# Long attention steps taken head by head, and value products of one step at a time in two column quarters

## The reference, cut to what matters

```python
# x: (4, 512, 512); a cross attention over 64 context rows comes first, then this layer,
# then a second cross attention and a second mixture of 32 experts
def attention(x, kv_d_w, q_d_w, k_u_w, v_u_w, q_u_w, rope_k_w, rope_q_w, o_w):
    # q, k, v: 16 heads of 32, half of each rotary
    ...
    scores = jnp.einsum('bqhd,bkhd->bhqk', q, k) * scale
    scores = jnp.where(causal[None, None], scores, jnp.finfo(scores.dtype).min)
    probs = jax.nn.softmax(scores, axis=-1)
    out = jnp.einsum('bhqk,bkhd->bqhd', probs, v).reshape(b, s, H)
    return out @ o_w

h = x + attention(rmsnorm(x, ln1_w), ...)
out = h + moe(rmsnorm(h, ln2_w), ...)     # one shared and 7 routed experts, top 2
```

## Time and profile before

| | |
|---|---|
| median of the three runs | 2032.91 us (2032.46 to 2034.27) |
| the profiled execution | 2038.68 us, its span 2036.5 us |
| busy over the span | PE 1606.6 us, DVE 1354.6, ACT 1017.8, POOL 884.9 |
| mean granted clock of PE | 0.869 of 2.4 GHz |
| attention of `front`, first scores to last products | some 142 to 655 us of the span |
| one value-product record (L1047) | 273 ns, median of 1280 |

### The profile page before, as it was taken

The page is one execution under the profiler, slowest core; times in us unless marked ns, Lnnn a source line. Parts: engine busy times, 40 slices in busy tenths (PEclk is TensorE's granted clock), DMA queues, the critical chain, the costliest instruction groups (busy, mean ns, idle before and its releaser), DMA issues. The chain is left out here.

```text
span 2036.5 us, 33507 instructions
## 1 busy us (share of the span) xinstructions
PE 1606.6 (79%) x8846; PEld 1224.0 (60%) x8847; DVE 1354.6 (67%) x2659; ACT 1017.8 (50%) x1941; POOL 884.9 (43%) x654
## 2 busy tenths in 40 slices
PE   4568697797776669999947652199999999999991
PEld 3445565565455447777726441188888888878881
DVE  7645665565564456667656432189999999999992
ACT  1124534434343046666511100178888888888880
POOL 4100010110201222444413556557887888788881
PEclk8589998898888779999965555599999999999996
DMA  9144234242240253675562113268888888898778
GB/s 324 39 103 105 65 107 99 63 134 53 63 125 1 92 154 101 159 164 102 83 200 76 42 35 94 59 145 178 177 194 183 180 174 201 192 225 202 127 125 278
DMA packets 170842, 266.19 MB, mean 131 GB/s; under 512 B 21856, under 2 KB 97504, under 8 KB 169024
## 3 DMA queue, kind: packets, MB, share of 16 engines
q0 software_dynamic: 52624, 113.84, 28.8%
q1 hardware_dynamic: 118128, 151.24, 25.0%
HBM read 150.55 MB, written 87.33 MB: 117 GB/s over the span
## 5 line engine op out<-in xcount | busy, mean ns | idle before, releaser
L1544 DVE TENSOR_TENSOR moe_w_lo<-moe_w_up,moe_w_hi 128x1536 fp32r<-128x1536 f32 (+1 forms) x216 | 408.3, 1890 | 31.7 <-ACT moe_w_hi L1430 22.1
L1430 ACT ACTIVATE moe_w_hi<-moe_w_up 128x1536 fp32r (+3 forms) x216 | 343.1, 1589 | 20.5 <-SPq L1332 20.5
L1371 POOL DMA_INDIRECT moe_rows<-moe_rows,moe_ids x200 | 317.4, 1587 | 68.2 <-issue 56.4
L1639 PE MATMUL psum<-moe_w_hi,moe_rows_hi 128*128 128x384 f32 (+1 forms) x864 | 323.1, 374 | 18.4 <-DVE moe_rows_lo L1538 18.3
L1640 PE MATMUL psum<-moe_w_lo,moe_rows_hi 128*128 128x384 f32 (+1 forms) x864 | 304.1, 352 | 0.0
L1641 PE MATMUL psum<-moe_w_hi,moe_rows_lo 128*128 128x384 f32 (+1 forms) x864 | 303.7, 352 | 0.0
L1665 PE MATMUL psum<-moe_w_down,moe_hid_t 128*128 (+1 forms) x544 | 268.6, 592 | 1.8 <-DVE moe_tail_t L1532 1.2
L1387 POOL DMA_INDIRECT moe_sum<-moe_res,moe_ids x100 | 163.8, 1638 | 104.8 <-ACT moe_res L1467 54.6
L816 DVE TENSOR_REDUCE neg_top<-psum 128x1 f32<-128x128 f32 (+3 forms) x256 | 118.2, 484 | 126.1 <-PE psum L1028 125.9
L1387 POOL DMA_INDIRECT moe_other<-moe_res,moe_ids x100 | 162.6, 1626 | 88.2 <-ACT moe_res L1467 35.0
L1538 DVE TENSOR_TENSOR moe_rows_lo<-psum,moe_rows_hi 128x512 fp32r<-128x512 f32 x216 | 148.7, 689 | 54.8 <-issue 42.9
(11 more groups left out here) (270 smaller groups left out, 2925.1 us busy)
## 6 DMA issues: line engine op xcount, KB each, us to landing
moe_w_up<-in_L_ffn_w_gate SPq DMA_DIRECT2D x32, 384.0 KB
moe_w_up<-in_L_ffn_w_up SPq DMA_DIRECT2D x32, 384.0 KB
q_st<-q_hi SPq DMA_DIRECT2D x64, 128.0 KB, 2.6
k_st<-k_hi SPq DMA_DIRECT2D x64, 128.0 KB, 2.7
k_st<-k_lo SPq DMA_DIRECT2D x64, 128.0 KB, 2.7
q_st<-q_lo SPq DMA_DIRECT2D x64, 128.0 KB, 2.7
moe_w_down<-in_L_ffn_w_down SPq DMA_DIRECT2D x32, 256.0 KB
moe_w_down<-in_L_ffn_w_down SPq DMA_DIRECT2D x64, 128.0 KB
```

The lines of the kernel that those rows point to most:

```text
L1371: pool.indirect_dma_start(rows[u][:, :], None, d["rows"], bass.IndirectOffsetOnAxis(ids[:, t:t + 1], 0)).then_inc(gathered[u], 16)
L1430: sc.activation(w_hi[u % SPLITS][:, :], w_up[:, bass.ds(at * DC, DC), :].rearrange("p a n -> p (a n)"), ACT.Copy).then_inc(T["wh"], 1)
L1544: v.tensor_tensor(w_lo[u % SPLITS][:, :], w_up[:, bass.ds(at * DC, DC), :].rearrange("p a n -> p (a n)"), w_hi[u % SPLITS][:, :].bitcast(F ...
L1639: mm(ps[:, 2 + i, 0:2 * I], hi, w_h, start=(k == 0), stop=False)
```

## The change

A long step becomes two units, `(n, 0)` and `(n, 1)`, one a head; a short step stays one unit `(n, None)`. All three engines' lists now run over `UNITS`. The transposes of head 0 go to bank 4, which DVE copies, those of head 1 to bank 5, which ACT copies. `prob_t` has three buffers. `attend(n)` does one step, two units after it, and so two heads in two column quarters at a time. The turned denominators go to bank 3 except at a batch's end, and copying them and scaling are two calls. Scores come two units ahead and ahead of all else in a unit. `between`'s pieces of the long half move by one step later (that part of the diff is left out; no piece changes). A small constant, `mean_w`, moves into the stage that uses it.

```diff
@@ -44,9 +44,8 @@
 NS = len(STEPS)
-def wide_steps(s):
-
-    return sum(i >= 2 for i, _ in STEPS[:s])
+UNITS = [(n, e) for n in range(BATCH * NS) for e in ((None,) if STEPS[n % NS][0] < 2 else (0, 1))]
+LAST_UNIT = {n: at for at, (n, e) in enumerate(UNITS)}
...
@@ -562,7 +561,7 @@
         rot_a, rot_b = sb("rot_a", [P, 2 * HEADS, ROT]), sb("rot_b", [P, 2 * HEADS, ROT])
         neg_top = sb("neg_top", [P, 2, 2])
         prob = sb("prob", [P, 2, 2, SEQ])
-        prob_t = sb("prob_t", [P, 2, 2 * TPB, P])
+        prob_t = sb("prob_t", [P, 3, 2 * TPB, P])
         den = sb("den", [P, TPB, HEADS])
         over_den = sb("over_den", [P, HEADS, HD])
         hn_t = sb("hn_t", [P, TPB, DC, P])
@@ -580,9 +579,28 @@
         LAST, ALL = BATCH - 1, BATCH * NS
         PHASE = NS // 2
         ends = lambda n: n % PHASE >= PHASE - 2
-        attends = lambda n: 2 * (n // 2 + 1)
+        attends = lambda n: n + 1
         is_wide = lambda n: STEPS[n % NS][0] >= 2
         nth = lambda i: QUERY_ORDER.index(i)
+        heads_of = lambda n, e: (0, 1) if e is None else (e,)
+        block_of = lambda n, e, j: e * (TPB if is_wide(n) else STEPS[n % NS][0] + 1) + j
+
+        def copied_first(n):
+
+            b, s = divmod(n, NS)
+            return b * (NS + PHASE) + (s + 1 + min(s + 1, PHASE))
+
+        def copied_second(n):
+            b, s = divmod(n, NS)
+            return b * PHASE + max(0, s + 1 - PHASE)
+
+        at_unit = {"den": {}, "den_flip": {}, "den_out": {}, "scaled": {}}
+        for n in range(ALL):
+            if ends(n):
+                later = (1, 2, 3, 5 if is_wide(n) else 4) if n % 2 == 0 else (1, 2, 3, 3) if is_wide(n) else (2, 3, 4, 4)
+                for name, lag in zip(at_unit, later):
+                    at_unit[name].setdefault(LAST_UNIT[n] + lag, []).append(n)
+        DEN_BANK = lambda n: 5 if n % NS == NS - 1 else 3
...
@@ -679,22 +697,23 @@
         def _(act):
             sc = nc.scalar
-            def exponents(n):
+            def exponents(n, e):
                 b, s = divmod(n, NS)
                 (i, hp), u = STEPS[s], s % 2
                 if n >= 2:
-                    act.wait_ge(S["pt"], n - 1)
-                for e in range(2):
+                    act.wait_ge(S["pt"], 2 * (n - 2) + heads_of(n, e)[-1] + 1)
+                for e in heads_of(n, e):
                     act.wait_ge(S["ntop"], 2 * n + (e + 1 if is_wide(n) else 2))
                     sc.activation(prob[:, u, e, 0:(i + 1) * P], score_at(n, e, (i + 1) * P), ACT.Exp, bias=neg_top[:, u, e:e + 1],
                                   accum_out=den[:, i, 2 * hp + e:2 * hp + e + 1]).then_inc(S["pexp"], 1)
             def prob_t_second(n):
-                act.wait_ge(S["pt"], n + 1)
-                act.wait_ge(S["pv"], attends(n - 2))
-                w = (STEPS[n % NS][0] + 1) * 2 * P - 512
-                sc.activation(prob_t[:, n % 2, 4:4 + w // P, :].rearrange("p c q -> p (c q)"), ps[:, 5, 0:w], ACT.Copy).then_inc(S["ptb"], 1)
+                act.wait_ge(S["pt"], 2 * n + 2)
+                if n >= 3:
+                    act.wait_ge(S["pv"], attends(n - 3))
+                w = STEPS[n % NS][0] + 1
+                sc.activation(prob_t[:, n % 3, TPB:TPB + w, :].rearrange("p c q -> p (c q)"), ps[:, 5, 0:w * P], ACT.Copy).then_inc(S["ptb"], 1)
             def z_out(b, t):
...
@@ -791,13 +810,15 @@
                     keys_out(0, t - 1)
             queries_out(0, LAST)
             keys_out(0, LAST)
-            for n in range(ALL):
-                exponents(n)
-                if n >= 1:
-                    if is_wide(n - 1):
-                        prob_t_second(n - 1)
-                    between((n - 1) // NS, (n - 1) % NS)
-            prob_t_second(ALL - 1)
+            for at in range(len(UNITS) + 1):
+                if at < len(UNITS):
+                    exponents(*UNITS[at])
+                if at >= 1:
+                    n, e = UNITS[at - 1]
+                    if e == 1:
+                        prob_t_second(n)
+                    if e != 0:
+                        between(n // NS, n % NS)
             for t in range(TPB):
                 hidden_out(LAST, t)
...
@@ -807,20 +828,20 @@
             v = nc.vector
             own = Steps(dve, S["dve"], 0, m["passed"]["dve"])
-            def maxima(n):
+            def maxima(n, e):
                 u, cols = n % 2, (STEPS[n % NS][0] + 1) * P
-                for e in range(2):
+                for e in heads_of(n, e):
                     dve.wait_ge(S["st"], 2 * n + (e + 1 if is_wide(n) else 2))
                     if n >= 2:
                         dve.wait_ge(S["pexp"], (n - 2) * 2 + e + 1)
                     v.tensor_reduce(neg_top[:, u, e:e + 1], score_at(n, e, cols), AX.X, ALU.max, negate=True).then_inc(S["ntop"], 1)
             def prob_t_first(n):
-                w = min(512, (STEPS[n % NS][0] + 1) * 2 * P)
-                dve.wait_ge(S["pt"], n + 1)
-                if n >= 2:
-                    dve.wait_ge(S["pv"], attends(n - 2))
-                v.tensor_copy(prob_t[:, n % 2, 0:w // P, :].rearrange("p c q -> p (c q)"), ps[:, 4, 0:w]).then_inc(S["pta"], 1)
+                w = (STEPS[n % NS][0] + 1) * (1 if is_wide(n) else 2)
+                dve.wait_ge(S["pt"], 2 * n + (1 if is_wide(n) else 2))
+                if n >= 3:
+                    dve.wait_ge(S["pv"], attends(n - 3))
+                v.tensor_copy(prob_t[:, n % 3, 0:w, :].rearrange("p c q -> p (c q)"), ps[:, 4, 0:w * P]).then_inc(S["pta"], 1 if is_wide(n) else 2)
             def denominators(n):
                 b, i = n // NS, STEPS[n % NS][0]
@@ -831,13 +852,17 @@
                 own.run(v.reciprocal(den[:, i, :], den[:, i, :]))
                 v.tensor_copy(over_den[:, :, :], den[:, i, :].unsqueeze(2).to_broadcast([P, HEADS, HD])).then_inc(S["rden"], 1)
-            def attended(n):
+            def denominators_out(n):
+                b, i = n // NS, STEPS[n % NS][0]
+                tile = b * TPB + nth(i)
+                dve.wait_ge(S["oproj"], b * TPB)
+                dve.wait_ge(S["rdt"], tile + 1)
+                v.tensor_copy(att_t[:, i].rearrange("p c q -> p (c q)"), ps[:, DEN_BANK(n), :]).then_inc(S["rdts"], 1)
+
+            def scaled(n):
                 b, i = n // NS, STEPS[n % NS][0]
                 tile = b * TPB + nth(i)
                 at = att_t[:, i].rearrange("p c q -> p (c q)")
-                dve.wait_ge(S["oproj"], b * TPB)
-                dve.wait_ge(S["rdt"], tile + 1)
-                v.tensor_copy(at, ps[:, 5, :]).then_inc(S["rdts"], 1)
                 dve.wait_ge(S["pv"], attends(n))
                 dve.wait_ge(S["rdts"], tile + 1)
...
@@ -981,18 +1006,21 @@
             keys_rest(0, LAST)
             for t in range(TPB):
                 normed(1, t)
-            maxima(0)
-            for n in range(ALL + 2):
-                if n + 1 < ALL:
-                    maxima(n + 1)
-                if 1 <= n <= ALL:
-                    prob_t_first(n - 1)
-                if n >= 2 and ends(n - 2):
-                    attended(n - 2)
-                if 1 <= n <= ALL:
-                    if ends(n - 1):
-                        denominators(n - 1)
-                    between((n - 1) // NS, (n - 1) % NS)
+            maxima(*UNITS[0])
+            for at in range(len(UNITS) + 4):
+                if at + 1 < len(UNITS):
+                    maxima(*UNITS[at + 1])
+                if 1 <= at <= len(UNITS) and UNITS[at - 1][1] != 1:
+                    prob_t_first(UNITS[at - 1][0])
+                for n in at_unit["den_out"].get(at, ()):
+                    denominators_out(n)
+                for n in at_unit["scaled"].get(at, ()):
+                    scaled(n)
+                for n in at_unit["den"].get(at, ()):
+                    denominators(n)
+                if 1 <= at <= len(UNITS) and UNITS[at - 1][1] != 0:
+                    n = UNITS[at - 1][0]
+                    between(n // NS, n % NS)
             for n in range(TPB):
                 residual(LAST, n)
...
@@ -1032,41 +1060,40 @@
                 b, s = divmod(n, NS)
                 if s == 0:
                     pe.wait_ge(S["vs"], TPB * (b + 1))
-                pe.wait_ge(S["pta"], n + 2)
+                pe.wait_ge(S["pta"], copied_first(n))
                 if is_wide(n):
-                    pe.wait_ge(S["ptb"], b * wide_steps(NS) + wide_steps(s + 2))
-                if s % PHASE == 0 and n > 0:
+                    pe.wait_ge(S["ptb"], copied_second(n))
+                if s % PHASE < 2 and n >= PHASE:
                     pe.wait_ge(S["attd"], (n // PHASE) * 2)
-                for j in range(STEPS[s][0] + 1):
-                    for at in (s, s + 1):
-                        i, hp = STEPS[at]
-                        for e in range(2):
-                            k, g = divmod(2 * hp + e, GH)
-                            cols = slice((2 * hp + e) * HD, (2 * hp + e + 1) * HD)
-                            if j <= i:
```

(118 more changed lines are left out.)

## The result

The changed kernel took 1974.30 us (median of 4 runs, 1966.42 to 1975.41) against 2033.59 us before on the same chip: ratio 0.9691 [0.9653, 0.9728], 59 us faster. The forecast was 2005. The profiled execution took 1975.16 us, its span 1973.2 against 2036.5: 63 us less.

The account below looks back on a forecast made before the run. Waits between engines were taken to bound the long halves, TensorE the short halves of batches 1 and 2. Terms -35 + 12 + 2 - 7 = -28 us gave 2005 us, 8-in-10 range 1985 to 2032.

Parts of the forecast that it names:

- The long halves, -35: Long halves of all four batches: units remove waits between engines, 28 us in batches 0 to 2 and 7 in batch 3.
- the start of a half, +2: At a half's start value products wait for the previous step's scaling on VectorE: 0.5 us a batch, bounds 0 and 8.
- the mismatch of 0.4 us a pair: Long pairs: two equally full in-order engines don't mesh fully, so 0.4 us is added, making a pair 5.6 us.
- rival 2: Each long step's value products wait for ScalarE's copy, up to 0.5 us plus queueing: 2050 us, chance 0.12.
- the signs named: Long halves near 52 us in batch 0, 58 to 62 elsewhere; wrong if VectorE exceeds 97% busy with TensorE waiting.
- Waves of 0.11 us: Value-product bursts on TensorE: a wave costs 0.11 us whether it fills four column quarters or two; +0.87 us a long pair.
- Batches 0 to 2 pay it in full, since TensorE there is dense: Short halves: a second burst costs +0.42 us a pair, 3.4 a half; with 2 for batch 3, +12 us.
- The clock, -7: Half-speed time in three long halves costs 23 us; a fuller TensorE returns a third, 7 us, bounds -8 and 23.
- the fourth: Rival in which everything meshes and the clock stays full: -35 + 12 + 2 - 23 = -44 us, 1989, chance 0.08.
- the other three: Rivals: in-order coupling, 2025, chance 0.15; products waiting for ScalarE's copy, 2050, 0.12; clock falling more, 2017, 0.10.

Follow-up runs that it names:

- The first experiment: Changed kernel with value products of two steps at once in four quarters again, units, banks and three buffers kept: 1955.21 us, ratio 0.9619.
- The second experiment: Kernel before with only the value products changed, to one step at a time in two quarters, no units, two buffers: 1999.51 us, ratio 0.9826.
- filler run: Kernel before with extra products in TensorE's waits of long pairs but each half's first: 2038.62 us (three waves meant per wait), 2035.96 (one).

## Why the prediction was wrong

The direction was right, and so was the mechanism in the long halves; the size was half: -28 us forecast, -59 measured (-63 in the profiled execution). What failed is the step on the short halves, and the clock was mis-sized. By its own terms:

- **The long halves, -35, and the start of a half, +2: right.** At 0.44 us for a us of half speed, the four halves shrank by 9.5, 8.0, 8.1 and 7.5 us at like clock, 33 in all, as the two terms together. So the sum comes out, but in part by luck, as two errors inside it cancel: the mismatch of 0.4 us a pair was 0 in all plain pairs (5.17; 4.73 in batch 3) but the first behind the rotary ones (0.6 in batch 0), and the products wait longer for the scaling at a half's start:

```profile
PE psum L1073 <- DVE att_t L868: 9.7, 4, 2.7
PE psum L1055 <- ACT prob L707: 9.1, 4, 7.1
```

That view of after, 150 to 600 us (us in total, times, longest), gives 2.4 us a time where 0.5 was charged; the products' wait for ScalarE's copy, which rival 2 put at each step, is there once, 0.7 us, and its 2050 falls. Of the signs named, the long halves came at 54.80, 56.48 and 58.19 us (52 and 58 to 62 forecast), and a plain pair with VectorE over 97% busy and TensorE waiting is seen, the first one (5.78 of 5.82 us), but not in the pairs behind it.

- **Waves of 0.11 us: right.** Bursts took 1.07 and 0.85 us, forecast 1.05 and 0.83. The Trainium skill's rule that changing the tiling mode drains TensorE ("TensorEngine Tiling (Array Packing)", Key Properties) is in this price: twice the switches. The first experiment gives 3.2 to 3.7 us in each short half of batches 0 to 2 for a forecast 3.4, but pair by pair it is 0 to 0.7 us for a forecast 0.42, and the burst's new place is in it, so the near agreement is partly luck.

- **The step that failed: the short halves, "Batches 0 to 2 pay it in full, since TensorE there is dense", +12.** TensorE wasn't dense in the sense the step needed. A busy share of 0.94 (60.57 of 64.70 us) hid waits of the old order, and a second burst falls into them at no cost. The second experiment, which adds the second bursts to the old order and nothing else, shows it. TensorE at the value projections (`w_vu`) of one pair in batch 1's short half, in the old order without the lists, with one-step products in the old order, and after:

```profile
297.00 1.02 PE L1100 MATMUL psum<-w_vu,kv_d 128*128 128x512 f32 x2
...
298.18 0.39 PE L1066 MATMUL psum<-const_sb,prob 128*128 128x128 f32 x2
298.80 0.67 PE L1086 MATMUL psum<-w_q,q_d 128*128 128x256 f32 x2 [0.24 <-ACT v_sb L711]
...
303.53 1.02 PE L1100 MATMUL psum<-w_vu,kv_d 128*128 128x512 f32 x2
```

```profile
290.38 1.02 PE L1100 MATMUL psum<-w_vu,kv_d 128*128 128x512 f32 x2
...
291.65 0.41 PE L1045 MATMUL psum<-prob_t,v_sb 128*32 128x128 f32 x4
291.99 0.44 PE L1066 MATMUL psum<-const_sb,prob 128*128 128x128 f32 x2
292.27 0.60 PE L1086 MATMUL psum<-w_q,q_d 128*128 128x256 f32 x2
...
296.91 1.02 PE L1100 MATMUL psum<-w_vu,kv_d 128*128 128x512 f32 x2
```

```profile
288.87 1.02 PE L1129 MATMUL psum<-w_vu,kv_d 128*128 128x512 f32 x2
...
295.40 1.02 PE L1129 MATMUL psum<-w_vu,kv_d 128*128 128x512 f32 x2
```

The pair takes 6.53 us in all three, all at full clock: before, the next projection waits for ScalarE's copy of the values, and the burst of four records at 291.65 stands in that wait. With four-quarter products behind the units the pair takes 6.02, since there the one burst stands in it. All eight pairs of that half, from a pair's first exponential to the next pair's, in us (one entry fell at a lower clock and is left out):

| pair | old order, no lists | old order, one-step | after, no lists |
|---|---|---|---|
| 1 | 5.55 | 5.78 | 4.00 |
| 2 | 15.58 | 15.58 | 15.63 |
| 3 (output projection) | 9.00 | 9.48 | 9.48 |
| 4 (output projection) | 9.44 | 9.93 | 9.93 |
| 5 | 6.53 | 6.53 | 6.53 |
| 6 | 3.94 | 3.95 | 3.95 |
| 7 | 4.76 | 4.76 | 4.81 |
| 8 | 7.50 | | 7.96 |

Pairs 3 and 4 pay the price, 0.48 us each for a forecast 0.42, and pair 8 pays 0.46 after; pairs 2, 5, 6 and 7 pay 0.05 at most. The units add a gain of their own at the half's start: pair 1 is 1.6 us shorter. Without the lists, the four short halves together went from 222.8 to 219.8 us, at a full clock by 4.5 us, where the step had +12. The profile hides such waits because the modelled end of each record (0.27 us long, the next 0.11 behind) covers the first part of them.

- **What no term held: transfers that make instructions late, some 6 us at like clock, 11 with the clock that goes with them, and the pause at the end of attention.** The prediction took 655 us as the end of attention and gave no term to the 7.36 us behind it. While GpSimd sends a batch's lists in eight indirect transfers 1.27 us apart, other engines' instructions start late. Timeline of before, the end of attention:

```profile
653.81 0.28 PE L1047 MATMUL psum<-prob_t,v_sb 128*32 128x128 f32 x2
...
656.63 0.95 POOL L275 DMA_INDIRECT moe_slots<-entry,slot  x1 [0.30 <-issue]
659.18 0.69 DVE L843 TENSOR_TENSOR att_t<-psum,att_t 128x512 f32<-128x512 f32 x1 [5.29 <-remote]
...
660.54 1.12 PE L1017 MATMUL psum<-const_sb,over_den 128*128 128x128 f32 x4 [6.45 <-DVE over_den L832]
...
661.45 1.06 PE L1119 MATMUL psum<-w_o,att_t 128*128 128x512 f32 x1
```

VectorE starts only 2.5 us after the last transfer's issue, TensorE stands behind it, and the end waits 7.36 us. After, the transfers meet the end too, but less hangs on what they hold up:

```profile
598.25 0.96 POOL L274 DMA_INDIRECT moe_slots<-entry,slot  x1 [0.30 <-issue]
...
598.39 0.85 PE L1073 MATMUL psum<-prob_t,v_sb 128*32 128x128 f32 x12 [0.67 <-ACT prob_t L716]
...
599.66 1.88 PE L1146 MATMUL psum<-w_o,att_t 128*128 128x512 f32 x4
```

The runs without the lists show the cost, by the medians 20 us and 9. Their profiles, at a full clock and up to the end of attention, show some 15 and 10; most of the difference is the pause at the end (7.36 us before, 1.91 without lists, 0.42 after either way). Why less is lost isn't settled further: the runs with later lists show only that the place by itself isn't it.

- **The clock, -7: too small, and the least certain.** Half-speed time in the halves fell by 37 us; at 0.44, about 16 us (12 to 14 at the 0.33 to 0.37 of the filler run), and 2 more in the pause at the end. The price has a third witness: batch 1's short half took 64.71 us at 0.96 and, without the transfers of later batches, 62.31 at 1.00, 0.46 for each us. What brought the clock back is open. Filling the waits, the prediction's reason, did raise the clock of the long halves in the filler runs; but four-quarter products behind the units, with TensorE less busy, had less half-speed time still (29 us), so a fuller TensorE isn't the whole of it. The Trainium skill's rule that activity releases the throttled state ("TensorE: Matmul & The Clock Gate", Part 1) agrees with the long halves of the filler runs, and doesn't tell by itself why the run with less work had the higher clock.

The account, for the 63 us between the two profiled executions, each term at a full clock and the clock by itself: long halves 33, clock 18, short halves 7, the pause at the end 5. Of the last two, 12 together, 6 are left when neither kernel sends the lists, so the transfers are the other 6. Against the forecast's -35 + 12 + 2 - 7: the long halves as forecast, the short ones 19 us off, the clock 11, and 5 in no term. The 33, 7 and 5 are read from the profiles; the 18 is an estimate from the price of 0.44.

Of the rivals, the fourth (everything meshes, clock full, 1989) came nearest; the other three, all slower than the forecast, fell. But it comes near by another road: it has the full 23 of the clock and the short halves at +12, and the measured clock gave 18 and the short halves gained. The range's lower end, 1985, left no room for short halves that gain, nor for the pause at the end.

## What to carry to other kernels

A change of two parts isn't the sum of each on the kernel before: price the second on the timeline that the first leaves, and think of each part alone, since here one gained 35 us alone and cost 19 to 25 behind the other. A stage with an engine 94% busy by the profile can still hold waits that take in a burst of 0.4 us a pair, so compare starts of like instructions, not busy shares. And look at the long idle times at a stage's ends before forecasting its middle: those marked as remote, beside another engine's small transfers, were worth 6 to 11 us against a forecast of 28.

## What the runs showed of the hardware

- Small indirect transfers issued by GpSimd delay the start of instructions on engines that have no part in them. Beside the 5.29 us above, in before's timeline TensorE's value products, elsewhere 0.11 us apart, came one by one, 0.7 us apart, with "issue" as what they waited for:

```profile
394.88 0.27 PE L1047 MATMUL psum<-prob_t,v_sb 128*32 128x128 f32 x1 [0.82 <-issue]
...
395.31 0.96 POOL L275 DMA_INDIRECT moe_slots<-entry,slot  x1 [0.30 <-issue]
395.59 0.27 PE L1047 MATMUL psum<-prob_t,v_sb 128*32 128x128 f32 x1 [0.44 <-issue]
...
396.35 0.27 PE L1047 MATMUL psum<-prob_t,v_sb 128*32 128x128 f32 x1 [0.49 <-issue]
```

24 such transfers cost 20 us in one kernel and, by medians that aren't clear of noise, 9 in the other. By which path they do isn't shown.

- More matmul work in the waits of one stretch raised its own granted clock (0.88 to 0.99). The stretch behind it, after a pause of TensorE of 8.39 us beside GpSimd's transfers, had a lower one (0.91 to 0.84). Half-speed time fell from 84 to 70 us in all, at no gain in time.
- Two or four column quarters filled, a wave of 128-column float32 products took 0.11 us: 28 records in one burst took 1.07 us, 16 and 12 of them in two bursts 1.07 and 0.85 us.
